# A two-layer attention and feed-forward kernel: column pieces in the opening, an earlier first group, key sums moved

## The reference

```python
x = x + mlstm(layernorm(x), ctx, ctx)        # 16 heads of 32, 16 sequences of 128 rows, 512 columns
x = x + ffn(layernorm(x))                    # rmsnorm, 8 routed experts (top 2) and a shared one
x = x + xattn(layernorm(x), ctx)             # 16 heads of 128; keys and values are made from ctx:
    k = rms_norm(ctx @ ki_w + ki_b, nki_s)   # mean of squares over all 2048 columns of a row
    v = ctx @ vi_w + vi_b
x = x + x @ ternary(weight).T + bias
```

## Time and profile before

| what | value |
|---|---|
| median of 3 runs | 1330.21 us (1328.85 to 1332.8) |
| the profiled execution: its time | 1327.5 us |
| the profiled execution: its span in the trace | 1325.8 us |
| PE busy | 1272.9 us, 96% |
| DVE, ACT, POOL busy | 840.4, 739.3, 391.7 us |
| mean granted TensorE clock | 0.993 of full speed |

### The profile page before, as it was taken

How to read it: one execution, slowest core, us unless ns; L and a number is a source line. 1 busy time by engine, 2 the same in 40 slices (tenths; PEclk the granted TensorE clock), 3 DMA queues, 4 the chain that set the end, 5 groups by cost and what they waited for, 6 DMA issues and landing times. The chain is left out here.

```text
span 1325.8 us, 24459 instructions
## 1 busy us (share of the span) xinstructions
PE 1272.9 (96%) x7380; PEld 1056.3 (80%) x7381; DVE 840.4 (63%) x1611; ACT 739.3 (56%) x1829; POOL 391.7 (30%) x363
## 2 busy tenths in 40 slices
PE   7999997998999899999999999999999999999998
PEld 6787875776777778788877778878888888888987
DVE  3644647778679863544445577463587777777965
ACT  5225538788886441445555455554786556556551
POOL 0111015273728016599531332163010000000041
PEclk9999999999999899999999999999999999999999
DMA  7897399887865394665669776555375565555403
GB/s 251 306 365 257 133 319 347 264 274 249 280 213 183 68 359 171 221 189 174 205 206 317 238 267 191 180 192 192 119 231 162 157 165 158 158 170 153 120 26 127
DMA packets 165831, 277.06 MB, mean 209 GB/s; under 512 B 29744, under 2 KB 57136, under 8 KB 165488
## 3 DMA queue, kind: packets, MB, share of 16 engines
q1 hardware_dynamic: 139648, 219.46, 51.8%
q0 software_dynamic: 8960, 30.41, 7.0%
q10 hardware_dynamic: 17136, 26.09, 5.3%
HBM read 167.11 MB, written 108.80 MB: 208 GB/s over the span
## 5 line engine op out<-in xcount | busy, mean ns | idle before, releaser
L121 PE MATMUL banks<-of_shared_split,key_lead 128*128 128x512 f32 x256 | 104.6, 409 | 6.7 <-DVE key_trail L1427 6.3
L3019 ACT ACTIVATE prob<-banks,attend_row,rq 128x128 f32<-128x128 f32 x248 | 110.5, 470 | 0.0
L3032 ACT ACTIVATE attend_ol<-banks,of_attend_vbias 128x512 fp32r<-128x512 f32 x64 | 44.2, 691 | 116.5 <-PE banks L3231 116.5
L121 PE MATMUL banks<-wo,attend_ol 128*128 (+1 forms) x256 | 106.2, 415 | 0.0
L121 PE MATMUL banks<-queries_rows_split,queries_wl 128*128 128x512 f32 x256 | 100.9, 394 | 0.2 <-DVE queries_rows_split L2655 0.2
L123 PE MATMUL banks<-wo,attend_ot 128*128 (+1 forms) x256 | 100.7, 393 | 0.0
L123 PE MATMUL banks<-of_shared_split,key_trail 128*128 128x512 f32 x256 | 100.6, 393 | 0.0
L122 PE MATMUL banks<-of_shared_split,key_lead 128*128 128x512 f32 x256 | 100.1, 391 | 0.0
L122 PE MATMUL banks<-wo,attend_ol 128*128 (+1 forms) x256 | 99.9, 390 | 0.0
L123 PE MATMUL banks<-queries_rows_split,queries_wt 128*128 128x512 f32 x256 | 99.8, 390 | 0.0
L122 PE MATMUL banks<-queries_rows_split,queries_wl 128*128 128x512 f32 x256 | 99.8, 390 | 0.0
(11 more groups left out here) (407 smaller groups left out, 3507.3 us busy)
## 6 DMA issues: line engine op xcount, KB each, us to landing
mlstm_gmax<-running_max SPq DMA_DIRECT2D x32, 512.0 KB, 6.4
k_heads<-heads_key ACTq DMA_DIRECT2D x64, 256.0 KB, 4.9
q_heads<-queries_head SPq DMA_DIRECT2D x64, 256.0 KB, 2.8
q_ahead<-q_heads SPq DMA_DIRECT2D x64, 256.0 KB, 4.1
of_attend_k<-k_heads SPq DMA_DIRECT2D x60, 256.0 KB, 4.0
of_attend_v<-v_heads SPq DMA_DIRECT2D x60, 256.0 KB, 3.3
key_raw<-in_L_xattn_ki_w SPq DMA_DIRECT2D x20, 512.0 KB, 5.8
sorted_rows<-of_shared_split SPq DMA_DIRECT2D x2, 5120.0 KB, 27.3
```

The source lines that it names most:

```text
L121: nc.tensor.matmul(out, lead_l, lead_r, start=first, stop=False)
L3019: ins = nc.scalar.activation(prob[:, j % 2, b, :], ps[:, j % 2, b * S:(b + 1) * S], ACT.Exp, bias=row[:, j % 2, 1, b:b + 1], scale=rq[:, b ...
L3032: nc.scalar.activation(ol[:, par, j, :], ps[:, 4 + j % 2, :], ACT.Identity, bias=vbias[:, bass.ds(quad_of(it) * 4 + j, 1)]).then_inc(ol_do ...
```

## The change

Values' opening: setup is no phase any more but the head of POOL's list in Values. Context group 0 is loaded as four column pieces of 256 KB (runs of 512 bytes), each ahead of its weight chunk. PE runs ten transposes of the identity into a bank that nobody reads, turns chunks 0 and 1, and turns chunk c + 2 behind `first_chunk(c)`; group 1's four turns stand together ahead of the last chunk. ACT takes the copies of units 0 and 2 one place sooner. The second column block's trails begin at unit 11 instead of 10. Heads: in group 0 the key units move one place ahead (three of them stay), with a raw weight load ahead of the body, and DVE's first products with scores stand among the context sums. End: 12 of the 16 sums of squared keys stand behind the last four key units (three each), four ahead of the third tail unit; ACT keeps the third tail unit behind the last root, and DVE adds the last square before the last group's heads are scaled.

```diff
-        TRAILS = {OPENS[q + 1] - (6 if q < QUADS - 2 else 5) + c: (q + 1, c) for q in range(QUADS - 1) for c in range(C)}
+        TRAILS = {OPENS[q + 1] - (6 if 0 < q < QUADS - 2 else 5) + c: (q + 1, c) for q in range(QUADS - 1) for c in range(C)}
...
-            load_ctx(0)
             for c in range(C):
+                sp.dma_start(stage[0][:, :, c * P:(c + 1) * P],
+                             a["ctx_2048"][0:GB, :, c * P:(c + 1) * P].rearrange("b s d -> s b d")).then_inc(ctx_first[c], 16)
                 sp.dma_start(raw[:, c, :], w_dram[c * P:(c + 1) * P, 0:N]).then_inc(first_loaded[c], 16)
             load_ctx(1)
...
+            setup(nc, K, pool, blank, made)
...
+            keep_even(0)
             turn_plain(C)
+            keep_even(2)
             turn_plain(C + 1)
-            keep_even(0)
-            keep_even(2)
...
-            for t in range(C):
-                turn(t)
+            pe.wait_ge(made, 1)
+            keep_busy(nc, ps[:, 0, :], K.ident, 10)
+            turn(0)
+            turn(1)
             for c in range(C):
                 first_chunk(c)
-                if c < C - 1:
-                    turn(C + c)
+                if c + 2 < C:
+                    turn(c + 2)
                 if c == C - 2:
-                    turn(C + c + 1)
+                    for t in range(C, 2 * C):
+                        turn(t)
...
-    OPENING = (0, 1, 2, 3, 5, 6, 8, 9, 11, 12, 14, 15)
+    OPENING = (-1, 0, 1, 2, 3, 5, 6, 8, 9, 11, 13, 15)
...
             load_q(0, 2)
+            next_raw(0, 1)
             body(0, True)
...
-            for b in range(TAIL_IN_HEADS):
+            for b in range(TAIL_IN_HEADS - 1):
                 keep_tail(b)
             act.wait_ge(sums, 1)
...
             nc.scalar.activation(K.rstd[:, EARLY:], K.mv[:, EARLY:, 1], ACT.Sqrt, bias=K.eps5[:, 0:1]).then_inc(late_root, 1)
+            keep_tail(TAIL_IN_HEADS - 1)
...
-            for b in range(GB):
-                context_sum(0, b)
+            context_sum(0, 0)
+            context_sum(0, 1)
             decayed(0, 0, True)
+            context_sum(0, 2)
+            context_sum(0, 3)
+            decayed(0, 1, True)
...
             factor(last)
+            finish(PER)
             dve.wait_ge(fac_done, G)
...
+            pe.wait_ge(total_done, CLOSES[G - 2] + 1)
+            pe.wait_ge(c_done, UNITS)
             for m in range(PER - LAG, PER):
                 keys(G - 1, m)
+                token_sums(range(3 * (m - PER + LAG), 3 * (m - PER + LAG) + 3))
...
+                if b == TAIL_IN_HEADS - 1:
+                    pe.wait_ge(total_done, UNITS)
+                    token_sums(range((G - 1) * GB, B)).then_inc(sums, 1)
```

More of the change, by code:

```diff
@@ L129, in keep_busy @@
         nc.tensor.transpose(bank[:, 0:P], ident[:], ident[:])
+def keep_busy(nc, bank, ident, n):
+    for _ in range(n):
+        nc.tensor.transpose(bank[:, 0:P], ident[:], ident[:])
 class RowStats:
@@ L160, in root, with setup @@
                                   ).then_inc(self.rooted, 1)
[L164 to L179, removed]
+def setup(nc, K, pool, blank, made):
+    nc.gpsimd.memset(K.ident[:], 0.0).then_inc(blank, 1)
+    nc.gpsimd.memset(K.ones[:], 1.0)
+    nc.gpsimd.memset(K.eps5[:], 1e-5)
+    nc.gpsimd.memset(K.eps6[:], 1e-6)
+    pool.wait_ge(blank, 1)
+    nc.gpsimd.affine_select(out=K.ident[:], in_=K.ident[:], compare_op=ALU.not_equal, fill=1.0,
+                            base=0, pattern=[[-1, P]], channel_multiplier=1).then_inc(made, 1)
 class Gates:
@@ L236, in values_and_gates @@
         product, even_done, odd_done = sem("product"), sem("even_done"), sem("odd_done")
+        blank, made = sem("blank"), sem("made")
+        ctx_first = [sem(f"ctx_first{c}") for c in range(C)]
         cleared, masks = sem("cleared"), sem("masks")
@@ L593, in turn @@
                 g, c = divmod(t, C)
-                if c == 0:
+                if g == 0:
+                    pe.wait_ge(ctx_first[c], 16)
+                elif c == 0:
                     pe.wait_ge(ctx_loaded[g], 16)
@@ L1220, in body @@
                         gather(g, n // 4)
-                    if n + 1 < PER or g + 1 < G:
+                    if (n + 1 < PER or g + 1 < G) and not (first and n < 3):
                         decayed(g, n + 1, first)
+                    if first and n == 0:
+                        decayed(g, 2, first)
                     if first:
                         keys_at(g, n, 1, weight_trail, first)
+                    if first and n == 1:
+                        decayed(g, 3, first)
                     if n % 4 == 0:
@@ L1292, in _ @@
             own(ins)
-            finish(PER)
             out = sq[:].rearrange("p (b h) e -> p b (h e)", b=GB)
@@ L1372, in _, with token_sums @@
                 body(g, False)
+            def token_sums(tokens):
+                for b in tokens:
+                    ins = nc.tensor.matmul(ps[:, 2, b:b + 1], total[:, b * S:(b + 1) * S], K.ones[:, 0:1],
+                                           start=True, stop=True)
+                return ins
+            pe.wait_ge(total_done, CLOSES[G - 2] + 1)
+            pe.wait_ge(c_done, UNITS)
             for m in range(PER - LAG, PER):
                 keys(G - 1, m)
+                token_sums(range(3 * (m - PER + LAG), 3 * (m - PER + LAG) + 3))
             pe.wait_ge(tail_loaded, 32)
@@ L3354, in two_layers @@
         K.stats, K.mv, K.rstd = kept("stats", [P, B, 6]), kept("mv", [P, B, 2]), kept("rstd", [P, B])
-        setup(nc, K)
         routed_weights = [a[f"L0_ffn_w_{n}"] for n in ("gate", "up", "down")]
```

## The result

| | median us | lowest to highest | runs | profiled execution: its time, span |
|---|---|---|---|---|
| before | 1330.78 | 1327.82 to 1336.16 | 9 | 1327.5, 1325.8 |
| after | 1337.38 | 1334.78 to 1341.47 | 9 | 1339.78, 1338.1 |

A forecast was written before the change was run, and what follows sets the result against it. PE, busy 96% of the span, was taken as the bound; opening -1.0, trails -2.35, heads' first group +1.2 and end of heads +0.5 gave -1.65 us, so 1328.6 us, range 1324.3 to 1332.8.

The forecast's parts named there:

- the price of heads' part: Heads' first group: PE about 2 us ahead, but the last split context part lands 1.4 us later; 1.2 us lost.
- The queue of heads' first group grows: Rival, chance 0.10: raw loads issued sooner in a full queue delay unit 10; at the bound +6.1 us, 1336.3.
- its bound of 9: Worst case for heads' first group: a transfer takes 14.4 us against 5.5, so 9 us lost.
- Values' 3.35: Values' forecast gain, 1.0 us from the opening and 2.35 from the trails, taken to go with transfers to heads.
- the 1.4: Heads' first group: raw weights issued ahead push back the last split part by 0.52 MB at 0.372 MB per us.
- Opening: Start of Values: first issue 0.8, first turn 4.5, first product 7.7, unit 4 at 23.45; 1.0 us gained.
- the 3.24 of the prediction: Opening of Values: 3.24 us from the first piece's landing to the first product, taken over from the old profile.
- the cold opening: Rival, chance 0.08: gaps between transposes leave the first products slow, 1.35 us dearer; change -0.3 us, 1329.9.
- Trails: Second weight block in Values: trails one unit later remove PE's whole wait at 52.14; 2.35 us gained.
- Heads' waits ahead: Heads' first group: of PE's 3.11 us wait before 203.18, some 1.3 us stays.
- that list is the same length: Heads' first group: scores at 227.77 follow DVE's list, without a gap from 218.5 on, so PE's lead isn't kept.
- End of heads: End of heads: the third tail copy, 0.60 us, stands behind the last root; 0.5 us lost (0.3 to 0.6).

## Why the prediction was wrong

The failed step is the price of heads' part: "they push it back by 0.52 MB at 0.372 MB per us, 1.4 us" and, from it, "I take **1.2 us lost**". The place, the transfer and the cause were the ones named, but the size was not. Heads' group lost 7.5 us in the profile (9.3 alone) and 6.9 us by the runs with and without that part. The second rival, "The queue of heads' first group grows", to which I gave 0.10, is what happened, toward its bound of 9. By its own scale, though, it needed unit 10 to start 7 us later for a loss of over 0.3%; counted from heads' start it came 6.04 us later. The loss passed 0.3% all the same, since the clock added 1.46 and only 1.67 of Values' 3.35 arrived. Three things were missing in the 1.4. I charged only the bytes issued ahead of the last part by one transfer's size over the whole rate, as if a queue were served strictly in order; it held PE until 9.65 us behind its issue (before 6.0), and still 7.5 us with the raw load behind it. From the scores of place 10 to unit 10 that made 4.07 us. By the end of the wait PE's clock had dropped: unit 10 took 1.46 us longer, which I had not priced. And I had put nothing on the way to the scores of place 10, where 1.97 us went. A bound that comes from a row with the same full queue (14.4 us for another block) deserved more than one chance in ten.

The other steps:

- **Opening.** First issue 0.82 (0.8 predicted), first product 7.08 (7.7), first turn 3.86 (4.5): the first piece, of 512-byte packets, was there no later than 3.86. Missed was the 1.48 us for the second piece: from the first turn to the first product it took 3.22 us, and that this is the 3.24 of the prediction is luck, since that was the time of sixteen transposes and this is eight and a wait. Waits of 0.18 and 0.37 us stood where 0.8 was expected, and none was listed before turn 8 (0.45). Unit 4 gained 1.89, not 1.0, when the clock was up. In five of the six profiles that have the ten idle transposes and the gap it was not, at 1.2 to 1.6 us, so the cold opening, given 0.08, was the common case.
- **Trails.** -2.35 agrees with the run of the trails alone (-2.3 us by the ratio, not clear of zero). Combined with the opening, a wait of 1.84 us came at unit 16.
- **"every transfer ahead of heads is issued behind some PE step, so the 3.35 of Values go with it."** This failed. PE's start moved, SP's queue did not: the gate loads held SP 2.55 us longer, and the second weight block was issued at 33.39 for 33.21. And DVE stood 2.37 us for an x load ahead of the third trail. Of the 1.89 and 2.35, 1.67 arrived at heads, and without heads' part the change measured as none (0.9994).
- **Heads' waits ahead.** 1.90 us where 1.3 was expected before 203. The scores of place 10 were to keep their distance from the group's start ("that list is the same length"); they came 1.97 us further behind it, and 1.84 with heads' part alone (36.43). That they stand where they stood before, 228.07 for 227.77, is Values' gain used up. No run separates the units' new places from DVE's new order here, so which of the two takes these 1.9 us is open.
- **End of heads.** +0.53, predicted +0.5.

## What to carry to other kernels

Where DMA is full, moving one load ahead of another is not priced by its bytes: here 0.52 MB ahead was priced at 1.4 us, and the part took 3.6 us longer, some 2 of them through that load. Give the longest issue-to-landing time seen in that queue a real share of the chances, and ask of every load that is moved sooner which PE step waits for the one it overtook. A gain at the start of a PE-bound phase reaches its end only if the loads due later are issued by the same clock; look where the next weights land before adding gains up. And a copy on an idle engine cost nothing ahead of the wait here (1.18 us), and 0.52 us behind it (1.70).

## What the runs showed of the hardware that was not expected

- **The opening's clock is not fixed by the code.** The same opening gave products 0.23 us apart in after and 0.43 in the kernel without heads' part, with gaps of 1.48 and 1.96 us before the second turn. The length of the gap doesn't order it: with gaps of 0.93, 1.27, 1.44 and 1.59 us the other four profiles of this opening had six to eight slow products. Even the old opening, which starts fast in the earlier trace rows, had its first product 0.57 us and its second 0.43 ahead of the next one in the trails' kernel. The granted clock column read 1.00 in these stretches all the same, so it was the spacing that told.
- **The clock in a wait.** In after, PE stopped at about 233.7; the granted clock averaged 0.91 over 234 to 238 and 0.50 over 238 to 242, that is 1.2 GHz, and unit 10 began there.
- **SP is held by its own issues.** The last two x loads of Values took 7.79 us to issue in after, while one piece of context took 0.43. Before, the same two took 2.79 us, with DMA as full (1.03 of its engines' time from 33 to 47 us before, 1.02 after), so a full DMA alone doesn't explain it; the cause is open:

```profile
37.42 7.79 SPq L259 DMA_DIRECT2D x_kept<-in_x  x2
```
